# Delta-rule scan on one core: output products kept for eight chunks and summed by TensorE, rounds unrolled

## The chip, the cores and the metric

The kernel runs on one core of one Trainium2 chip. The metric is the device time of one execution in microseconds (us); lower is better. Five engines work side by side and meet only at semaphores: TensorE (PE in the profile), VectorE (DVE), ScalarE (ACT), GpSimd (POOL) and SyncE (SP, which here only issues DMAs).

## The reference

The program is a small model of several blocks: a gated-experts layer, a gated delta-rule attention, gated experts again, a prototype mixture, a helical attention and a second mixture. The change touches the recurrence of the delta-rule attention alone. For each of 2 x 16 heads it walks 2048 time steps with a 16x16 state S:

```python
def step(S, inp):
    qt, kt, vt, at, bt = inp
    v_hat = jnp.einsum('bij,bi->bj', S, kt)
    err = vt - v_hat
    S = at[:, None, None] * S + bt[:, None, None] * (kt[:, :, None] * err[:, None, :])
    o = jnp.einsum('bij,bi->bj', S, qt)
    return (S, o)
_, O = lax.scan(step, S0, (Q.swapaxes(0, 1), Kh.swapaxes(0, 1), V.swapaxes(0, 1), alpha.T, beta.T))
```

S goes from step to step, so the walk is serial; o is read out at each step and feeds nothing in the walk.

## The kernel before

Before the scan, other stages write one record of small matrices for each chunk of 8 steps (C = CHUNK = 8). With these a chunk needs only the state before it: an error vector, a triangular solve giving u, the next state, and the outputs. The scan (`delta_recurrence`) runs over 32 rounds of 64 steps (SPAN = 64), each of 8 chunks (`m` = 0 to 7), so 256 chunks. The partitions hold 2 batches x 16 heads x 4 quarters; each partition has 4 columns j of the state (JQ = 4). Records and values of a round sit in one of two buffers, `slot` 0 or 1, and a `Fori` loop on every engine runs over the 16 pairs of rounds.

**VectorE** carries the serial chain. One chunk is six links (`at` = 0 to 5), and each link is issued for two lanes of 2 columns: products `terms` from the record and the state; a reduce to `error`; products `u_terms`; a reduce to `u`; products `s_terms`; a reduce to the new `state`. The products are `tensor_tensor` with two SBUF inputs (line 1798), the reduces have one input (lines 1810, 1814, 1818). Each link counts its lane's semaphore `chain[lane]` up by one, and the next link waits for it. Between links 4 and 5 VectorE also reduces the outputs of the chunk before (`outputs`, line 1794), and those of chunk 7 after the last link of the round.

**GpSimd** forms the outputs, in four instructions a chunk, all `tensor_tensor`. The first, below called product A, is released by the state of the chunk before, the same event that releases link 0 of VectorE. The second, product B, is released by u, the same event that releases link 4:

```python
nc.gpsimd.tensor_tensor(o_terms[:, m % 2, :, :, 0:HD], state..., Q_IN part of the record, ALU.mult)   # A, line 1773
nc.gpsimd.tensor_tensor(o_terms[:, m % 2, :, :, HD:], u..., MIX part of the record, ALU.mult)        # B, line 1777
```

Each output has 16 + 8 = 24 products. Two adds fold them to 12 (`o_halves`, line 1781) and to 6 (`o_quarters`, line 1785), and VectorE reduces the 6.

**ScalarE** writes the decayed old state into `s_terms` (line 1761, once a chunk, before link 5) and copies the round's values into `terms` (line 1757). **SyncE** loads two rounds ahead: when a round's outputs are complete it issues their store (two DMAs) and then the record and values of the round that takes over the slot (four DMAs). **TensorE** has nothing in this stage. After the scan come a barrier of all engines and `delta_output`, which reads the outputs back.

## Time and profile before

| what | us |
|---|---|
| median of 3 runs | 5733.3 (5731.94 to 5738.86) |
| the profiled execution, its own time | 5734.14 |
| span of the profile | 5732.2 |
| VectorE busy over the span | 4562.1 (80%) |
| GpSimd busy over the span | 2916.3 (51%) |
| TensorE busy over the span | 3463.3 (60%) |
| ScalarE busy over the span | 2952.6 (52%) |

The shares are means over stages that have little in common. The scan is the stretch from about 918 us to 2230 us. A stretch of it is read from the timeline (each line an instruction, or several alike in a row on one engine), and the groups of instructions by line give means over all chunks.

### The profile page before, as it was taken

How to read it: one execution, taken by the hardware profiler on the slowest of the kernel's cores; microseconds unless marked ns; L12 is line 12 of the kernel's file. 1: busy time of each engine (PE TensorE's matmuls, PEld its weight loads, DVE VectorE, ACT ScalarE, POOL GpSimd, SP SyncE). 2: the span in 40 equal slices, each digit the busy share in tenths (PEclk: the TensorE clock that was granted, in tenths of full speed). 3: DMA queues.
4: the chain of work that ended last, by engine and by line, in shares of the span. 5: the costliest groups of instructions: out<-in, count | busy, mean ns of one | idle time of the engine just before them, and what ended most of it. 6: DMA issues, size and time to landing. Idle time of an engine off the chain costs nothing. (4 is left out here: it accounts for less than half of the span.)

```text
span 5732.2 us, 66648 instructions
## 1 busy us (share of the span) xinstructions
PE 3463.3 (60%) x14606; PEld 1230.7 (21%) x14606; DVE 4562.1 (80%) x8093; ACT 2952.6 (52%) x3700; POOL 2916.3 (51%) x2351
## 2 busy tenths in 40 slices
PE   7972000000000002888975899999999999999568
PEld 3330000000000001332332233333333333333123
DVE  5554776999999997553487899999999999999352
ACT  5563000101001002553445598989898988999632
POOL 1001564777777774112045366666666666666512
PEclk9996555555555556998998799999999999999889
DMA  1016324223232322000124211111111111110200
GB/s 40 11 35 119 65 25 107 64 52 66 49 66 49 66 52 76 10 14 0 58 99 166 49 35 33 32 33 33 33 32 33 32 33 34 41 37 5 80 27 30
DMA packets 143838, 275.50 MB, mean 48 GB/s; under 512 B 73808, under 2 KB 87504, under 8 KB 136336
## 3 DMA queue, kind: packets, MB, share of 16 engines
q1 hardware_dynamic: 142128, 263.57, 19.9%
q10 hardware_dynamic: 1440, 8.65, 0.4%
q8 instruction: 129, 2.11, 0.2%
q14 instruction: 141, 1.16, 0.1%
HBM read 178.65 MB, written 93.36 MB: 47 GB/s over the span
## 5 line engine op out<-in xcount | busy, mean ns | idle before, releaser
L1027 POOL TENSOR_TENSOR att_heads_rest<-att_heads_probs,att_heads_high 128x576 f16<-128x576 f32 x1024 | 1390.7, 1358 | 848.2 <-ACT att_heads_high L1114 842.1
L1144 DVE TENSOR_REDUCE att_heads_maxima<-att_heads_peek 128x1 f32<-128x512 f32 x2048 | 1311.2, 680 | 99.2 <-PE att_heads_peek L1040 72.2
L1112 ACT ACTIVATE att_heads_probs<-att_heads_scores 128x1024 f32<-128x1024 f32 x1024 | 1076.2, 1051 | 248.9 <-PE att_heads_scores L1058 240.6
L1058 PE MATMUL att_heads_scores<-att_heads_q,att_heads_k 128*128 128x512 f16 (+1 forms) x4096 | 1067.8, 382 | 34.2 <-issue 21.2
L1882 PE MATMUL delta_out_sums<-delta_out_squares,main_head_sum 128*128 128x512 f32 x32 | 16.6, 649 | 1763.4 <-ACT delta_out_squares L1911 1763.4
L1114 ACT ACTIVATE att_heads_high<-att_heads_scores 128x1024 f16<-128x1024 f32 x1024 | 1077.5, 1052 | 0.0
L1164 DVE TENSOR_TENSOR att_heads_rest<-att_heads_probs,att_heads_high 128x448 f16<-128x448 f32 x1024 | 892.0, 871 | 65.2 <-POOL att_heads_rest L1027 53.1
L1040 PE MATMUL att_heads_peek<-att_heads_k,att_heads_q 112*128 112x512 f16 x2048 | 687.9, 395 | 89.4 <-DVE att_heads_maxima L1144 47.5
L1761 ACT ACTIVATE delta_scan_s_terms<-delta_scan_state,delta_scan_record 128x64 f32<-128x64 f32 x256 | 104.7, 409 | 1160.2 <-DVE delta_scan_state L1818 1160.2
L1058 PEld LDWEIGHTS att_heads_scores<-att_heads_q,att_heads_k 128*128 128x128 f16 (+1 forms) x4096 | 395.0, 98 | 455.3 <-ACT att_heads_high L1114 38.8
L1074 PE MATMUL att_heads_out<-att_heads_high,att_heads_v_head 128*64 128x512 f16 x2048 | 418.5, 405 | 5.1 <-DVE att_heads_rest L1164 4.2
L1074 PE MATMUL att_heads_out<-att_heads_rest,att_heads_v_head 128*64 128x512 f16 x2048 | 393.9, 381 | 0.0
L1882 PEld LDWEIGHTS delta_out_sums<-delta_out_squares,main_head_sum 128*128 128x128 f32 x32 | 6.6, 211 | 1772.3 <-issue 1772.3
L1574 POOL TENSOR_TENSOR delta_chunks_terms<-delta_chunks_kq 128x256 f32<-128x256 f32 (+3 forms) x64 | 157.1, 2479 | 422.5 <-DMA delta_chunks_ab<-delta_ab 402.0
L1773 POOL TENSOR_TENSOR delta_scan_o_terms<-delta_scan_state,delta_scan_record 128x512 f32<-128x512 f32 x256 | 341.5, 1334 | 29.8 <-DMA delta_scan_vt<-delta_v 29.3
L259 PE MATMUL ffn_pre<-ffn_xn_parts,ffn_weights 128*128 128x512 f16 x1536 | 336.0, 382 | 11.5 <-POOL ffn_weights L298 11.5
L1777 POOL TENSOR_TENSOR delta_scan_o_terms<-delta_scan_u,delta_scan_record 128x256 f32<-128x256 f32 x256 | 201.4, 787 | 241.4 <-DVE delta_scan_u L1814 241.4
L1798 DVE TENSOR_TENSOR delta_scan_terms<-delta_scan_record,delta_scan_state 128x256 f32<-128x256 f32 x512 | 300.8, 626 | 18.8 <-ACT delta_scan_terms L1757 15.0
L341 DVE SCALAR_TENSOR_TENSOR main_x<-ffn_hidden,ffn_gate,main_x 128x512 f32<-128x512 f32 x256 | 194.9, 764 | 151.1 <-ACT ffn_hidden L284 151.1
L1798 DVE TENSOR_TENSOR delta_scan_s_terms<-delta_scan_record,delta_scan_u 128x256 f32<-128x256 f32 x512 | 312.9, 650 | 0.0
L1040 PEld LDWEIGHTS att_heads_peek<-att_heads_k,att_heads_q 112*128 112x128 f16 x2048 | 160.0, 96 | 647.8 <-DVE att_heads_maxima L1144 549.2
L1781 POOL TENSOR_TENSOR delta_scan_o_halves<-delta_scan_o_terms 128x384 f32<-128x384 f32 x256 | 284.3, 1110 | 20.1
(240 smaller groups left out, 5174.0 us busy)
## 6 DMA issues: line engine op xcount, KB each, us to landing
delta_scan_record<-delta_record SPq DMA_DIRECT2D x64, 1026.0 KB, 10.7
att_heads_q<-att_hel SPq DMA_DIRECT2D x192, 128.0 KB, 3.1
att_heads_k<-att_hel SPq DMA_DIRECT2D x192, 128.0 KB, 3.3
delta_record<-delta_chunks_record SPq DMA_DIRECT2D x64, 256.5 KB, 4.7
att_hel<-att_hel_high SPq DMA_DIRECT2D x32, 512.0 KB, 3.9
att_hel<-att_hel_rest SPq DMA_DIRECT2D x32, 512.0 KB, 4.5
att_o<-att_heads_out_copy SPq DMA_DIRECT2D x256, 32.0 KB
att_out_parts<-att_o ACTq DMA_DIRECT2D x8, 1024.0 KB, 14.2
```

The lines of the kernel that those rows point to most:

```text
L259: mm = nc.tensor.matmul(pre[:, k % SLOTS], weights[:, u, w_part, tile, o * P:(o + 1) * P], xn_parts[:, x_part, tile, tokens(n)], start=til ...
L1027: nc.gpsimd.tensor_tensor(rest[:, step % 4, SPLIT:], probs[:, step % 4, SPLIT:], high[:, step % 4, SPLIT:], ALU.subtract).then_inc(rest_b_ ...
L1040: nc.tensor.matmul(peek[:, m % 2], q[0:MAX_ROW, slot, 0, tile * P:(tile + 1) * P], k[0:MAX_ROW, slot, 0, tokens(blk)], start=True, stop=Tr ...
L1058: mm = nc.tensor.matmul(scores[:, step % 2, tokens(j)], k[0:rows, slot, number, tile * P:(tile + 1) * P], q[0:rows, slot, number, tokens(h ...
L1074: mm = nc.tensor.matmul(out[j * WIDE:(j + 1) * WIDE, half], v_head[:, slot, tile], part[:, step % 4, tokens(j)], start=tile == 0 and part ...
L1112: nc.scalar.activation(probs[:, step % 4], scores[:, step % 2], ACT.Exp, scale=LOGIT_SCALE).then_inc(probs_ready, 1)
L1114: nc.scalar.activation(high[:, step % 4], scores[:, step % 2], ACT.Exp, scale=LOGIT_SCALE).then_inc(high_ready, 1)
L1144: nc.vector.tensor_reduce(maxima[:, m:m + 1], peek[:, m % 2], AX.X, ALU.max).then_inc(peek_read, 1)
L1164: nc.vector.tensor_tensor(rest[:, step % 4, 0:SPLIT], probs[:, step % 4, 0:SPLIT], high[:, step % 4, 0:SPLIT], ALU.subtract).then_inc(rest ...
L1773: nc.gpsimd.tensor_tensor(o_terms[:, m % 2, :, :, 0:HD], state[:, (m - 1) % 4].unsqueeze(2).broadcast_to([P, JQ, C, HD]), table[:, Q_IN:Q_ ...
L1781: nc.gpsimd.tensor_tensor(o_halves[:, m % 2], o_terms[:, m % 2, :, :, 0:FOLD], o_terms[:, m % 2, :, :, FOLD:], ALU.add).then_inc(o_halves_ ...
L1798: return nc.vector.tensor_tensor(out, matrix.rearrange("p (r c) -> p r c", c=columns).unsqueeze(1).broadcast_to([P, JL, rows, columns]), v ...
```

## The change

GpSimd keeps only the two products. `o_terms` grows from two chunks to two rounds of eight chunks, so the 24 products of all 64 steps of a round stay in SBUF. When GpSimd has finished a round, TensorE multiplies the identity matrix with each of the 24 product slices (256 columns, 24 elements apart in SBUF, float32) and accumulates them in half a PSUM bank, `o_sum`; two banks alternate. ScalarE copies the sum to `o_out` with one instruction (`evict`), placed in its queue after the decay of chunk 4 of the next round (EVICT_AT = 4). The store of a round, and the loads that follow it in SyncE's queue, wait for that copy. The two folding adds of GpSimd and the output reduce of VectorE go. VectorE gets one wait at link 3 for GpSimd's product A of three chunks before. All `Fori` loops over pairs of rounds are written out.

```diff
--- before.py
+++ after.py
@@ -1694,14 +1694,12 @@
         u_terms = s.sb("u_terms", [P, 2, JQ, C, C])
...
         s_terms = s.sb("s_terms", [P, 2, JQ, HD, C + 1])
-        o_terms = s.sb("o_terms", [P, 2, JQ, C, HD + C])
-        FOLD = (HD + C) // 2
-        o_halves = s.sb("o_halves", [P, 2, JQ, C, FOLD])
-        o_quarters = s.sb("o_quarters", [P, 2, JQ, C, FOLD // 2])
+        o_terms = s.sb("o_terms", [P, 2, CHUNKS, JQ, C, HD + C])
+        o_sum = s.ps("o_sum", [P, 2, BLK])
         o_out = s.sb("o_out", [P, 2, JQ, SPAN])
...
         stored = [s.sem(f"stored{slot}") for slot in range(2)]
-        o_halves_ready, o_quarters_ready = s.sem("o_halves_ready"), s.sem("o_quarters_ready")
+        o_summed = s.sem("o_summed")
         chain = [s.sem(f"chain{lane}") for lane in range(LANES)]
...
         ROUNDS = T // SPAN
@@ -1709,7 +1707,7 @@
         STEP = 6
...
         C0 = BEFORE + 1
-        O_CREDIT = 2 * CHUNKS
+        EVICT_AT = 4
 
...
             for lane in range(LANES):
@@ -1729,7 +1727,7 @@
 
...
 
-                    sp.wait_ge(o_ready, (pair * 2 + slot + 1) * CHUNKS + O_CREDIT)
+                    sp.wait_ge(o_ready, pair * 2 + slot + 1)
                     for b in range(B):
...
                         sp.dma_start(dram["delta_o"][b, bass.ds(pair * 2 + slot, 1)].rearrange("r (p j) t -> (r p) (j t)", j=JQ),
@@ -1737,18 +1735,26 @@
 
...
                     load(0, slot)
-                with sp.Fori(1, ROUNDS // 2) as pair:
+                for pair in range(1, ROUNDS // 2):
                     for slot in range(2):
...
                 for slot in range(2):
-                    sp.wait_ge(stored[slot], ROUNDS // 2 * 32 + 32)
+                    sp.wait_ge(stored[slot], ROUNDS // 2 * 32)
 
...
             def _(act):
-                with act.Fori(0, ROUNDS // 2) as pair:
+                def evict(round_number):
+                    slot = round_number % 2
+                    act.wait_ge(o_summed, round_number + 1)
+                    if round_number >= 2:
+                        act.wait_ge(stored[slot], round_number // 2 * 32)
+                    nc.scalar.activation(o_out[:, slot].rearrange("p j (m t) -> p m j t", t=C),
+                                         o_sum[:, slot, 0:CHUNKS * JQ * C].rearrange("p (m j t) -> p m j t", m=CHUNKS, j=JQ), ACT.Copy).then_inc(o_ready, 1)
+
+                for pair in range(ROUNDS // 2):
                     for slot in range(2):
...
 
@@ -1760,39 +1766,43 @@
                             wait_chains(act, ((pair * 2 + slot) * CHUNKS + m) * STEP + C0)
...
                                                  scale=record[:, slot, m, DECAY:DECAY + 1]).then_inc(decayed, 1)
+                            if m == EVICT_AT and pair * 2 + slot >= 1:
+                                evict(pair * 2 + slot - 1)
+                evict(ROUNDS - 1)
+
+            @block.tensor
+            def _(pe):
+                for round_number in range(ROUNDS):
+                    slot = round_number % 2
+                    pe.wait_ge(o_terms_ready, (round_number + 1) * CHUNKS * 2)
+                    if round_number >= 2:
+                        pe.wait_ge(o_ready, round_number - 1)
+                    by_element = o_terms[:, slot].rearrange("p m j t e -> p e (m j t)")
+                    for e in range(HD + C):
+                        mm = nc.tensor.matmul(o_sum[:, slot, 0:CHUNKS * JQ * C], c["identity"][:], by_element[:, e], start=e == 0, stop=e == HD + C - 1)
+                    mm.then_inc(o_summed, 1)
 
...
             def _(pool):
-                with pool.Fori(0, ROUNDS // 2) as pair:
+                for pair in range(ROUNDS // 2):
                     for slot in range(2):
                         pool.wait_ge(loaded[slot], (pair + 1) * LOADS)
+                        if pair >= 1:
+                            pool.wait_ge(o_summed, pair * 2 + slot - 1)
                         for m in range(CHUNKS):
...
                             wait_chains(pool, number * STEP + C0)
-                            nc.gpsimd.tensor_tensor(o_terms[:, m % 2, :, :, 0:HD], state[:, (m - 1) % 4].unsqueeze(2).broadcast_to([P, JQ, C, HD]),
+                            nc.gpsimd.tensor_tensor(o_terms[:, slot, m, :, :, 0:HD], state[:, (m - 1) % 4].unsqueeze(2).broadcast_to([P, JQ, C, HD]),
                                                     table[:, Q_IN:Q_IN + C * HD].rearrange("p (t i) -> p t i", i=HD).unsqueeze(1)
...
                             wait_chains(pool, number * STEP + C0 + 4)
-                            nc.gpsimd.tensor_tensor(o_terms[:, m % 2, :, :, HD:], u[:, m % 4].unsqueeze(2).broadcast_to([P, JQ, C, C]),
+                            nc.gpsimd.tensor_tensor(o_terms[:, slot, m, :, :, HD:], u[:, m % 4].unsqueeze(2).broadcast_to([P, JQ, C, C]),
                                                     table[:, MIX:MIX + C * C].rearrange("p (t s) -> p t s", s=C).unsqueeze(1)
                                                     .broadcast_to([P, JQ, C, C]), ALU.mult).then_inc(o_terms_ready, 1)
-                            pool.wait_ge(o_terms_ready, number * 2 + 2)
-                            nc.gpsimd.tensor_tensor(o_halves[:, m % 2], o_terms[:, m % 2, :, :, 0:FOLD], o_terms[:, m % 2, :, :, FOLD:], ALU.add
-                                                    ).then_inc(o_halves_ready, 1)
-                            pool.wait_ge(o_halves_ready, number + 1)
-                            pool.wait_ge(o_ready, number + O_CREDIT - 1)
-                            nc.gpsimd.tensor_tensor(o_quarters[:, m % 2], o_halves[:, m % 2, :, :, 0:FOLD // 2], o_halves[:, m % 2, :, :, FOLD // 2:],
-                                                    ALU.add).then_inc(o_quarters_ready, 1)
 
...
             def _(dve):
-                def outputs(pair, slot, m):
-                    dve.wait_ge(o_quarters_ready, (pair * 2 + slot) * CHUNKS + m + 1)
-                    if m == 0:
-                        dve.wait_ge(stored[slot], pair * 32 + 32)
-                    nc.vector.tensor_reduce(o_out[:, slot, :, m * C:(m + 1) * C], o_quarters[:, m % 2], AX.X, ALU.add).then_inc(o_ready, 1)
-
                 def product(out, matrix, vector, rows, columns):
                     return nc.vector.tensor_tensor(out, matrix.rearrange("p (r c) -> p r c", c=columns).unsqueeze(1).broadcast_to([P, JL, rows, columns]),
@@ -1822,21 +1832,17 @@
                     dve.sem_inc(chain[lane], BEFORE)
...
                     nc.vector.memset(state[:, 3, lane * JL:(lane + 1) * JL], 0.0).then_inc(chain[lane], 1)
-                dve.sem_inc(o_ready, O_CREDIT)
-                for slot in range(2):
-                    dve.sem_inc(stored[slot], 32)
-                with dve.Fori(0, ROUNDS // 2) as pair:
+                for pair in range(ROUNDS // 2):
                     for slot in range(2):
...
                             for at in range(STEP):
+                                if at == 3 and number >= 3:
+                                    dve.wait_ge(o_terms_ready, number * 2 - 5)
                                 if at == 5:
-                                    if m >= 1:
-                                        outputs(pair, slot, m - 1)
                                     dve.wait_ge(decayed, number + 1)
                                 link(slot, m, number, at)
-                        outputs(pair, slot, CHUNKS - 1)
 
...
```

## Rows read from the trace of the kernel before

**Rows 1.** Groups by line, 930 to 2227 us: busy us, mean ns, idle before.
```profile
L1773 POOL TENSOR_TENSOR delta_scan_o_terms<-delta_scan_state,delta_scan_record 128x512 f32<-128x512 f32 x256 | 341.5, 1334 | 29.8 <-DMA delta_scan_vt<-delta_v 29.3
...
L1781 POOL TENSOR_TENSOR delta_scan_o_halves<-delta_scan_o_terms 128x384 f32<-128x384 f32 x256 | 284.3, 1110 | 20.1
...
L1777 POOL TENSOR_TENSOR delta_scan_o_terms<-delta_scan_u,delta_scan_record 128x256 f32<-128x256 f32 x256 | 201.4, 787 | 241.4 <-DVE delta_scan_u L1814 241.4
...
L1761 ACT ACTIVATE delta_scan_s_terms<-delta_scan_state,delta_scan_record 128x64 f32<-128x64 f32 x256 | 104.7, 409 | 1160.2 <-DVE delta_scan_state L1818 1160.2
```

**Rows 2.** Timeline, first chunk into the second: start, us, engine, line, idle before.
```profile
935.12 0.48 DVE L1798 TENSOR_TENSOR delta_scan_u_terms<-delta_scan_record,delta_scan_error 128x128 f32<-128x128 f32 x2
935.52 0.47 DVE L1814 TENSOR_REDUCE delta_scan_u<-delta_scan_u_terms 128x16 f32<-128x128 f32 x2
935.90 0.74 DVE L1798 TENSOR_TENSOR delta_scan_s_terms<-delta_scan_record,delta_scan_u 128x256 f32<-128x256 f32 x2
936.57 0.80 DVE L1818 TENSOR_REDUCE delta_scan_state<-delta_scan_s_terms 128x32 f32<-128x288 f32 x2
937.29 0.75 DVE L1798 TENSOR_TENSOR delta_scan_terms<-delta_scan_record,delta_scan_state 128x256 f32<-128x256 f32 x2
937.96 0.77 DVE L1810 TENSOR_REDUCE delta_scan_error<-delta_scan_terms 128x16 f32<-128x272 f32 x2
938.65 0.59 DVE L1798 TENSOR_TENSOR delta_scan_u_terms<-delta_scan_record,delta_scan_error 128x128 f32<-128x128 f32 x2
```

**Rows 3.** Timeline, chunks 6 and 7 of the first round.
```profile
964.79 0.47 DVE L1814 TENSOR_REDUCE delta_scan_u<-delta_scan_u_terms 128x16 f32<-128x128 f32 x2
965.18 1.19 DVE L1798 TENSOR_TENSOR delta_scan_s_terms<-delta_scan_record,delta_scan_u 128x256 f32<-128x256 f32 x2
965.40 0.69 POOL L1777 TENSOR_TENSOR delta_scan_o_terms<-delta_scan_u,delta_scan_record 128x256 f32<-128x256 f32 x1 [0.88 <-DVE delta_scan_u L1814]
...
967.28 1.12 DVE L1798 TENSOR_TENSOR delta_scan_terms<-delta_scan_record,delta_scan_state 128x256 f32<-128x256 f32 x2
967.38 0.73 POOL L1785 TENSOR_TENSOR delta_scan_o_quarters<-delta_scan_o_halves 128x192 f32<-128x192 f32 x1 [0.16 <-POOL delta_scan_o_halves L1781]
```

**Rows 4.** Timeline, chunk 0 of the second round and the start of chunk 1.
```profile
973.00 1.25 POOL L1773 TENSOR_TENSOR delta_scan_o_terms<-delta_scan_state,delta_scan_record 128x512 f32<-128x512 f32 x1
...
976.27 0.75 DVE L1798 TENSOR_TENSOR delta_scan_s_terms<-delta_scan_record,delta_scan_u 128x256 f32<-128x256 f32 x2
976.49 1.11 POOL L1777 TENSOR_TENSOR delta_scan_o_terms<-delta_scan_u,delta_scan_record 128x256 f32<-128x256 f32 x1 [2.24 <-DVE delta_scan_u L1814]
...
977.66 0.75 DVE L1798 TENSOR_TENSOR delta_scan_terms<-delta_scan_record,delta_scan_state 128x256 f32<-128x256 f32 x2
977.68 1.58 POOL L1781 TENSOR_TENSOR delta_scan_o_halves<-delta_scan_o_terms 128x384 f32<-128x384 f32 x1
```

**Rows 5.** Timeline, chunks 6 and 7 of the second round.
```profile
1003.63 1.27 POOL L1773 TENSOR_TENSOR delta_scan_o_terms<-delta_scan_state,delta_scan_record 128x512 f32<-128x512 f32 x1
...
1005.17 0.47 DVE L1814 TENSOR_REDUCE delta_scan_u<-delta_scan_u_terms 128x16 f32<-128x128 f32 x2
...
1010.78 0.78 POOL L1777 TENSOR_TENSOR delta_scan_o_terms<-delta_scan_u,delta_scan_record 128x256 f32<-128x256 f32 x1 [0.89 <-DVE delta_scan_u L1814]
```

**Rows 6.** Windows on float32 matmuls, L689 (256 columns): PE, PEld, clock.
```profile
2866.00:2872.00 6.00, 6.00 (x28) 4.91 (x27) 1.00 0.44 175
```

**Rows 7.** Windows on the start of the next stage's float32 matmuls, all engines.
```profile
2249.50:2253.00 3.50, 3.46 (x5) 1.56 (x6) 0.00 (x0) 0.84 (x1) 0.00 (x0) 0.53 1.13 218
```

**Rows 8.** Timeline, the last of the four load DMAs after a round.
```profile
1502.63 0.48 SPq L1728 DMA_DIRECT2D delta_scan_vt<-delta_v  x1
```

**Rows 9.** The same DMA by its tile, 1502.6 to 1503.2 us: time to landing.
```profile
DMA to landing us min/median/max: 11.0/11.0/11.0
```

**Rows 10.** Timeline, end of the scan.
```profile
2224.54 0.80 DVE L1818 TENSOR_REDUCE delta_scan_state<-delta_scan_s_terms 128x32 f32<-128x288 f32 x2
...
2225.97 0.35 DVE L1794 TENSOR_REDUCE delta_scan_o_out<-delta_scan_o_quarters 128x32 f32<-128x192 f32 x1 [0.63 <-POOL delta_scan_o_quarters L1785]
```

## The prediction

> **What bounds the kernel now.** I first read the groups by line of the scan [rows 1]. GpSimd's products A and B and the first add come 256 times at 1.33, 0.79 and 1.11 us, and the second add took 0.73 us where the timeline shows it [rows 3]: about 4 us a chunk. ScalarE's single instruction a chunk had waited 1160 us in total for VectorE's new state [rows 1]. Then the timeline: the same reduce to u of chunk 6 starts at 964.79 in one round and at 1005.17 in the next [rows 3, 5], so a round is 40.38 us and a chunk 5.05 us. All other waits being short, VectorE's chain of links sets the pace. GpSimd is no bound by its own length, but see what it does to VectorE.
>
> VectorE's chunk without disturbance can be put together from the start times of the first chunks [rows 2]: terms 937.29 to error 937.96 is 0.67, to u_terms 938.65 is 0.69, u_terms 935.12 to u 935.52 is 0.40, to s_terms 935.90 is 0.38, to state 936.57 is 0.67, to the next terms 937.29 is 0.72. That sums to 3.53 us. Against 5.05, 1.52 us a chunk is something else. The output reduce is 0.34 to 0.35 long [rows 10] and overlaps its neighbours, some 0.26. The rest, over 1.2 us, is inside VectorE's products. A pair of s_terms products takes 0.74 or 0.75 us in [rows 2, 4] but 1.19 in [rows 3], a pair of terms 0.75 against 1.12 in the same groups. The reduces don't change (0.80, 0.77, 0.47). In each long pair a GpSimd product or add started after VectorE's first of two instructions and before the second: the two engines' two-input instructions exclude each other, and the pair is longer by what is left of GpSimd's.
>
> **Who wins.** The contested moment is that in which VectorE's first instruction of a pair is done. In [rows 3] B starts 0.22 after the s_terms pair, takes its own 0.69, and the pair takes 1.19: GpSimd went between the two. Of the 256 chunks, 192 look like this, all with GpSimd idle for 0.88 us before. In [rows 4] B starts 0.22 after the pair as well, but the pair takes 0.75 and B 1.11: VectorE went through and GpSimd waited. That is so in chunk 0 of all 32 rounds, where GpSimd had been idle 2.24 us. The contest right after it also goes to VectorE: the add starts 0.02 after the terms pair, takes 1.58 and the pair 0.75 [rows 4], while the other add against a terms pair wins [rows 3].
>
> **The change, part by part.**
> 1. *Output reduce off VectorE*: 0.26 us a chunk of the chain. Its replacement is counted below.
> 2. *Both adds off GpSimd*: 1.11 and some 0.7 a chunk [rows 1, 3]. Worth nothing by themselves; but they no longer collide with the terms pair and, through the queue, no longer push A into the u_terms pair.
> 3. *A moves*. Before, it stood behind the second add. Now GpSimd waits for the state, so A is released together with the terms pair, as B is with the s_terms pair, and by the same kind of event: I put its start 0.22 after the pair, as B's. A and B both meet a pair of VectorE head on, in every chunk.
>  - Price if GpSimd wins. For B, 1.19 against 0.75 is 0.44 where B takes 0.69; where B takes 0.78 [rows 5] it is 0.09 more. The two lengths come equally often, mean 0.49. In general it is GpSimd's time less 0.25. A takes 1.25 with nothing of VectorE beside it [rows 4], and in the other chunks some 0.17 less (1.27 where it waited about 0.18 for a pair [rows 5]). With a wait of 0.05 it costs 1.05 or 0.89, mean 0.98.
>  - Price if VectorE wins. B: nothing [rows 4]. A begins its work about 0.35 later, ends 1.65 to 1.85 after the chunk's start, and the u_terms pair is due at 0.67 + 0.69 = 1.36, so it must wait. In [rows 5] A ends at 1004.90 and the reduce to u starts at 1005.17, 0.27 later; undisturbed it starts at 1.76. So 0.16 or 0.36, mean 0.27.
> 4. *TensorE*: 24 float32 matmuls of 256 columns, two passes each. A window of such matmuls has 28 passes in 6.0 us at granted clock 1.00, 0.214 each [rows 6]; 48 are 10.3 us. Each round TensorE starts after some 25 us of rest, and the next stage's first 3.5 us after a rest ran at 0.53 of the 2.4 GHz [rows 7], half clock. I take 4 us at half clock (9 passes) and 39 x 0.214 = 8.3: 12.3 us. It lies beside the next round. The copy is asked for after chunk 4's decay, some 4 chunks and 1 us on, at 19 to 21 us, so cover remains. Below, all 48 at half clock is 20.6 us. No moving operand in the trace has a stride as here (96 bytes); if it cost twice the time, 25 us.
> 5. *ScalarE's copy*: 256 elements; the decay of 64 takes 0.41 [rows 1], I estimate 0.5 us. ScalarE is idle four fifths of each chunk.
> 6. *Loads later*. Store and loads now go out after chunk 4, not at the end of the round. From the copy, six issues of about 0.5 us up to the last [rows 8], which lands 11.0 us later [rows 9]: 14 us. With 1.2 us up to the copy's end and 0.8 for the copies of values it is 16 us after chunk 4's start; four chunks are 18 us at 4.5 a chunk. Hidden; at chunks under 4.0 us it isn't.
> 7. *Waits and loops*. The new wait of VectorE at link 3 is for a product three chunks back, satisfied long before. Written-out loops remove register and branch work that the intervals of [rows 2] don't show as a bound: 0.
> 8. *Tail*. Before, the last output is done at 2225.97 + 0.35 = 2226.32, 0.98 after the last state (2224.54 + 0.80) [rows 10]. Now TensorE starts about when B ends, 1.0 before the last state, and 12.3 + 0.5 + 0.3 for handovers bring it to 12.1 after it: +11 us, once.
>
> **Sum.** The change comes down to two contests. In the new queue GpSimd is idle before B from A's end to u: if A wins, A ends 1.5 after the chunk's start and B starts 1.0 (A's delay) + 2.14 + 0.22 = 3.4 after it, 1.9 idle. That is nearer to the 2.24 of the lost contest than to the 0.88 of the won ones, so I let B lose. Then B ends late, at most 0.3 us before A's release, so A has hardly rested and wins. A chunk is 3.53 + 0.98 = 4.51, a round 36.1, against 40.4: 4.3 x 32 = 137 us less. With the tail, -126. On the profiled execution's 5734.1 that gives 5608, and 5607 on the median of 5733.3 (the two differ by 0.8). I forecast **5607 us**, chance 0.36 together with its variant: after a lost contest GpSimd loses the next as well, as in [rows 4]. Then chunks alternate between 4.51 and 3.53 + 0.27 + 0.49 = 4.29, a round is 35.2, and the time 5578.
>
> The Trainium skill (SBUF — State Buffer, "SBUF: two separate sides") says that GpSimd and two-input VectorE instructions share a port pair by an exclusive lock, which goes for the whole instruction to whoever starts first. The 192 chunks like [rows 3] agree, the 32 like [rows 4] don't: there B starts 0.11 us before VectorE's second instruction and yet waits 0.4. By that rule the change would come out as the first rival does, at 5732.
>
> **Rivals.**
> - *GpSimd wins every contest* (0.34). Each chunk is 3.53 + 0.98 + 0.49 = 5.00, a round 40.0, 0.4 x 32 = 13 us less, and the tail takes 11 back: **5732**, no change. For it: 192 contests against 32 in the very geometry. If loss belongs to chunk 0 for a reason of its own, B still loses there: 0.53 x 32 = 17 us less, **5715**. I give 0.18 to the first and 0.16 to the second.
> - *VectorE wins against A, GpSimd against B* (0.12). A's rest is 1.1 us when B wins, B's then 0.9, so if the limit of rest lies below 1.1 this is stable: 4.29 x 8 = 34.3 a round, -195 + 11: **5550**.
> - *VectorE wins both* (0.04): 3.80 a chunk, 30.4 a round, but the loads (part 6) then bind at about 31.5: -284 + 11, **5460**.
> - *TensorE late* (0.14), the one on the slow side. ScalarE's queue holds the copy ahead of the decay of chunk 5, and link 5 of VectorE waits for the decay. If the strided reads double the matmul time to 25 us, the copy waits at 21 us, the decay comes 4 us late in each round, and with contests as in the first rival that is +128: **5860**. It decides from about 21 us for the 24 matmuls. Against it: 20.6 even at half clock throughout.
>
> **How the numbers follow.** From no change I can tell about 0.2%, 11.5 us. The range from 5545 to 5740 holds the forecast and its variant, the first rival in both forms, and the second: 0.82. Its bounds also take in A's price from 0.89 to 1.05 (21 us either way over 256 chunks). The forecast's own range is 5565 to 5630. Faster by over 0.2%: 0.36 + 0.12 + 0.04 + 0.16, and a little of the 5732 case, 0.70. Same: 0.15. Slower: 0.15, the TensorE case and a little of the 5732 case.
>
> **What the profile afterwards would show.** Product A starting 0.2 after the first terms product in all chunks; the terms pair 1.6 to 1.8 us long (A won) or 0.75 (A lost, and u_terms long); the s_terms pair 0.75 with B at 1.1 (B lost) or 1.2 (B won). 24 matmuls a round over about 12 us, the copy never waiting, no DMA wait at a round's start, and about 12 us between the last state and the last copy. I am wrong if who wins is set by something other than GpSimd's rest, if A's start moves past VectorE's second instruction, if TensorE needs over 20 us a round, or if VectorE's undisturbed intervals grow.

## The result and the profile after

The changed kernel takes 5820.35 us (median of 4 runs, 5809.46 to 5822.52) where the one before took 5732.62 in the same session: a ratio of 1.0148, interval 1.0130 to 1.0166. It is 1.5% slower; forecast were 5607 us, range 5545 to 5740. The profiled execution has a span of 5820.7 us against 5732.2.

The groups by line of the scan, 930 to 2325 us, answer to [rows 1]; the columns are the same.

```profile
L1782 PE MATMUL delta_scan_o_sum<-delta_scan_o_terms,main_identity 128*128 128x256 f32 x1536 | 993.6, 838 | 843.1 <-POOL delta_scan_o_terms L1800 843.1
...
L1808 DVE TENSOR_TENSOR delta_scan_terms<-delta_scan_record,delta_scan_state 128x256 f32<-128x256 f32 x512 | 416.4, 851 | 104.5 <-ACT delta_scan_terms L1763 104.5
...
L1796 POOL TENSOR_TENSOR delta_scan_o_terms<-delta_scan_state,delta_scan_record 128x512 f32<-128x512 f32 x256 | 314.7, 1229 | 391.9 <-DVE delta_scan_state L1828 257.7 <-DMA delta_scan_vt<-delta_v 127.0 <-DVE delta_scan_terms L1808 7.2
...
L1800 POOL TENSOR_TENSOR delta_scan_o_terms<-delta_scan_u,delta_scan_record 128x256 f32<-128x256 f32 x256 | 188.2, 735 | 492.0 <-DVE delta_scan_u L1824 492.0
```

Two things stand out. TensorE is busy for 993.6 us, 31.05 a round, where I had 12.3. And VectorE, which had waited for hardly anything, now waits 104.5 us ahead of its terms. The waits over the stage say for whom (engine, line, waited for, us in total, times, longest):

```profile
ACT delta_scan_o_out L1754 <- PE delta_scan_o_sum L1782: 260.1, 32, 34.8
...
ACT delta_scan_terms L1763 <- DMA delta_scan_vt<-delta_v: 240.9, 31, 35.0
...
DVE delta_scan_terms L1808 <- ACT delta_scan_terms L1763: 104.5, 31, 14.7
...
DVE delta_scan_state L1828 <- ACT delta_scan_s_terms L1767: 5.6, 7, 1.5
```

ScalarE waits for TensorE's sum in every round (34.8 of it at the end, the other 225 us in 31 rounds), then for loads, and VectorE waits for ScalarE. The timeline of one round shows the chain, from chunk 4 into the next round:

```profile
1507.84 1.27 DVE L1808 TENSOR_TENSOR delta_scan_s_terms<-delta_scan_record,delta_scan_u 128x256 f32<-128x256 f32 x2
...
1508.06 0.77 POOL L1800 TENSOR_TENSOR delta_scan_o_terms<-delta_scan_u,delta_scan_record 128x256 f32<-128x256 f32 x1 [1.90 <-DVE delta_scan_u L1824]
...
1509.76 1.64 DVE L1808 TENSOR_TENSOR delta_scan_terms<-delta_scan_record,delta_scan_state 128x256 f32<-128x256 f32 x2
...
1509.98 1.14 POOL L1796 TENSOR_TENSOR delta_scan_o_terms<-delta_scan_state,delta_scan_record 128x512 f32<-128x512 f32 x1 [1.15 <-DVE delta_scan_state L1828]
...
1511.34 0.38 ACT L1754 ACTIVATE delta_scan_o_out<-delta_scan_o_sum 128x256 f32<-128x256 f32 x1 [6.13 <-PE delta_scan_o_sum L1782]
...
1514.80 0.60 SPq L1726 DMA_DIRECT2D delta_scan_vt<-delta_v  x1
...
1523.79 6.73 PE L1782 MATMUL delta_scan_o_sum<-delta_scan_o_terms,main_identity 128*128 128x256 f32 x10 [12.48 <-POOL delta_scan_o_terms L1800]
...
1525.56 0.75 ACT L1763 ACTIVATE delta_scan_terms<-delta_scan_vt 128x64 f32<-128x64 f32 x4 [5.47 <-DMA delta_scan_vt<-delta_v]
...
1526.34 1.15 DVE L1808 TENSOR_TENSOR delta_scan_terms<-delta_scan_record,delta_scan_state 128x256 f32<-128x256 f32 x2 [1.61 <-ACT delta_scan_terms L1763]
...
1529.11 0.78 POOL L1800 TENSOR_TENSOR delta_scan_o_terms<-delta_scan_u,delta_scan_record 128x256 f32<-128x256 f32 x1 [2.24 <-DVE delta_scan_u L1824]
```

The copy (1511.34) had waited 6.13 us for the sum. Behind it SyncE issues the store and the four loads, the last at 1514.80; ScalarE can use their values 10.8 us later, at 1525.56, and VectorE has by then waited 0.8 of its 1.61 us for the new round. From the copy's start to the values it is 14.2 us, as estimated from [rows 8, 9]; but 14.2 after a sum that takes 31 is too late. The sum of round r starts at the end of r, and the loads behind it are those of round r + 2. So two rounds take the 39.5 us of a round's chunks, less 0.95 because the sum starts before the last state is done, plus 31.05 for the sum, 14.2 from copy to values and 0.8 for ScalarE's copies of the values: 84.6, or 42.3 a round. The two rounds that end at 1526.34 took 84.7; over the stage the way from copy to the new round is 15.4 on average instead of 15.0, and a round takes 42.6.

Products: B starts 0.22 after the s_terms pair, takes 0.77, and the pair 1.27; A starts 0.22 after the terms pair, takes 1.14, and the pair 1.64. GpSimd wins both. Of the 256 s_terms pairs 254 are lengthened in their second instruction, and 218 of the terms pairs: 472 contests won. Of the other 38 terms pairs, 31 are chunk 0 of a round, where the loads release A ahead of the pair (A was 0.7 us ahead at 1526.34), and in 5 A came 0.5 us after the pair's start, too late for a contest. At 1529.11, in chunk 0, B wins after 2.24 us of rest and with A run ahead of the terms pair: the very case in which it lost in [rows 4].

The two s_terms pairs and two terms pairs that are left are contests that GpSimd lost, and all four lie in the first chunks of the first round: B in chunks 0 and 2, after 2.24 and 1.90 us of rest, and A in chunks 1 and 3, after 0.28 and 0.37. In chunks 1 to 3 of that round the winner is just the one that the prediction's variant has: a B that has rested long loses, the A behind it, which has not rested, loses as well, and then GpSimd wins twice; chunks 1 and 2 take 4.19 and 4.43 us. From B of chunk 3 on GpSimd loses no contest, whatever its rest. Here is B in chunk 2 and in chunk 4, with the same start and the same rest:

```profile
945.13 0.74 DVE L1808 TENSOR_TENSOR delta_scan_s_terms<-delta_scan_record,delta_scan_u 128x256 f32<-128x256 f32 x2
945.35 1.02 POOL L1800 TENSOR_TENSOR delta_scan_o_terms<-delta_scan_u,delta_scan_record 128x256 f32<-128x256 f32 x1 [1.90 <-DVE delta_scan_u L1824]
...
954.19 1.27 DVE L1808 TENSOR_TENSOR delta_scan_s_terms<-delta_scan_record,delta_scan_u 128x256 f32<-128x256 f32 x2
954.41 0.77 POOL L1800 TENSOR_TENSOR delta_scan_o_terms<-delta_scan_u,delta_scan_record 128x256 f32<-128x256 f32 x1 [1.91 <-DVE delta_scan_u L1824]
```

What begins in the program between the last contest that GpSimd loses (A of chunk 3) and the first that it wins against this pattern (B of chunk 4) is VectorE's new wait at link 3, which is there from chunk 3 of the first round on (`at == 3 and number >= 3`).

The windows over one sum (busy us of PE, PEld, DVE, ACT and POOL, then granted clock, DMA share, GB/s), and the end of the stage against [rows 10]:

```profile
1480.00:1511.00 31.00, 30.75 (x48) 15.46 (x48) 27.00 (x65) 2.64 (x9) 11.13 (x12) 0.50 0.08 17
```
```profile
2290.80 31.05 PE L1782 MATMUL delta_scan_o_sum<-delta_scan_o_terms,main_identity 128*128 128x256 f32 x48 [12.21 <-POOL delta_scan_o_terms L1800]
2290.95 0.80 DVE L1828 TENSOR_REDUCE delta_scan_state<-delta_scan_s_terms 128x32 f32<-128x288 f32 x2
2321.89 0.38 ACT L1754 ACTIVATE delta_scan_o_out<-delta_scan_o_sum 128x256 f32<-128x256 f32 x1 [34.78 <-PE delta_scan_o_sum L1782]
```

48 passes in 30.75 us is 0.64 each, and the granted clock stays at 0.50 of 2.4 GHz though TensorE works without a pause. The last copy ends 30.5 us after the last state, where the last output was 0.98 after it before.

The account: the last state comes at 2291.75 instead of 2225.34, 66.4 later. That is 104.5 - 15.0 us of waiting for values (15.0 is the wait at the stage's start, which both have) plus 5.6 for the decay, less about 29 by which the chunks themselves are shorter (some 20 of them in chunk 0, 4.48 us long against 5.14 in experiment 2, because A has run ahead of the pair). The tail adds 29.5: 96. The later stages took 3498 us in this profile and 3506 in the one before, which makes the 88.5 of the two spans; in the profiles of this study they lie between 3492 and 3507, and no run here explains the spread.

### The profile page after: what moved, and what is told of

It reads as the page before. It is cut to its first block and busy times, and to the rows that moved or that the text cites. A ratio compares the mean times of both kernels' runs of the same rounds, so it can differ in the third digit from the quotient of the medians.

```text
span 5820.7 us, 65636 instructions
## 1 busy us (share of the span) xinstructions
PE 4448.1 (76%) x16142; PEld 1722.4 (30%) x16142; DVE 4555.4 (78%) x7837; ACT 2958.9 (51%) x3732; POOL 2429.2 (42%) x1839
## 5 line engine op out<-in xcount | busy, mean ns | idle before, releaser
L1782 PE MATMUL delta_scan_o_sum<-delta_scan_o_terms,main_identity 128*128 128x256 f32 x1536 | 993.6, 838 | 843.1 <-POOL delta_scan_o_terms L1800 843.1
L1144 DVE TENSOR_REDUCE att_heads_maxima<-att_heads_peek 128x1 f32<-128x512 f32 x2048 | 1310.1, 679 | 92.9 <-PE att_heads_peek L1040 66.4
L1782 PEld LDWEIGHTS delta_scan_o_sum<-delta_scan_o_terms,main_identity 128*128 128x128 f32 x1536 | 494.5, 324 | 1341.9 <-POOL delta_scan_o_terms L1800 879.5
L1808 DVE TENSOR_TENSOR delta_scan_terms<-delta_scan_record,delta_scan_state 128x256 f32<-128x256 f32 x512 | 416.4, 851 | 104.5 <-ACT delta_scan_terms L1763 104.5
L1796 POOL TENSOR_TENSOR delta_scan_o_terms<-delta_scan_state,delta_scan_record 128x512 f32<-128x512 f32 x256 | 314.7, 1229 | 391.9 <-DVE delta_scan_state L1828 257.7
L1800 POOL TENSOR_TENSOR delta_scan_o_terms<-delta_scan_u,delta_scan_record 128x256 f32<-128x256 f32 x256 | 188.2, 735 | 492.0 <-DVE delta_scan_u L1824 492.0
L284 ACT ACTIVATE ffn_hidden<-ffn_pre,ffn_expert 128x512 f32<-128x512 f32 x256 | 175.5, 687 | 138.7 <-PE ffn_pre L259 136.0
## 6 DMA issues: line engine op xcount, KB each, us to landing
delta_scan_record<-delta_record SPq DMA_DIRECT2D x64, 1026.0 KB, 10.8
```

Source lines behind the costliest of these rows:

```text
L1144: nc.vector.tensor_reduce(maxima[:, m:m + 1], peek[:, m % 2], AX.X, ALU.max).then_inc(peek_read, 1)
L1782: mm = nc.tensor.matmul(o_sum[:, slot, 0:CHUNKS * JQ * C], c["identity"][:], by_element[:, e], start=e == 0, stop=e == HD + C - 1)
L1796: nc.gpsimd.tensor_tensor(o_terms[:, slot, m, :, :, 0:HD], state[:, (m - 1) % 4].unsqueeze(2).broadcast_to([P, JQ, C, HD]), table[:, Q_IN: ...
L1808: return nc.vector.tensor_tensor(out, matrix.rearrange("p (r c) -> p r c", c=columns).unsqueeze(1).broadcast_to([P, JL, rows, columns]), v ...
```

## The experiments

**1. Contiguous reads.** Only what TensorE reads is changed; the sums are of the wrong products.

```diff
-by_element = o_terms[:, slot].rearrange("p m j t e -> p e (m j t)")
+by_element = o_terms[:, slot].rearrange("p m j t e -> p (m j t e)").rearrange("p (e n) -> p e n", e=HD + C)
```

> The kernel after, with one edit: each of the 24 matmuls of a round reads 256 consecutive floats of the round's products instead of every 24th, so the sums are of the wrong products; all instructions, waits and sizes stay. Theory 1, the 96-byte stride of the moving operand makes a pass take 0.64 us: a pass falls to 0.43 us (half clock) or 0.21 (full clock), the 48 passes of a round from 30.8 us to 10 to 21, the waits of ScalarE and GpSimd for loads at the start of a round (104.5 us of VectorE's waiting) vanish, and the tail after the last state shortens by 10 to 18 us: about 5700 to 5715. Rival, a pass over 256 float32 columns with the identity costs 0.64 us whatever it reads (the clock, the weight loads): no change, 5820.

Measured: 5724.65 us, ratio 0.9993 (0.9984 to 1.0003) to the kernel before: theory 1, 10 us above its range. The windows at the start of a sum and after:

```profile
1365.00:1370.00 5.00, 4.10 (x12) 3.40 (x13) 5.00 (x13) 0.41 (x1) 2.06 (x2) 0.60 0.01 3
1370.00:1378.00 8.00, 8.00 (x38) 6.72 (x36) 8.00 (x19) 0.82 (x2) 3.59 (x4) 1.00 0.00 0
```

The clock begins at half and is full from 3.1 us on in this sum (3 to 6 us in the others); 38 passes take 8 us, 0.21 each. In the last sum the 48 passes were 12.46 us busy, the 12.3 of the prediction. VectorE waits for values at the stage's start alone (14.4 us). So the strided operand is the whole of the slowdown, and what is left of the change is worth nothing measurable.

**2. Element outermost.** A complete version of the same: the layout puts each slice of 256 together, and GpSimd writes with a long stride.

```diff
-o_terms = s.sb("o_terms", [P, 2, CHUNKS, JQ, C, HD + C])
+o_terms = s.sb("o_terms", [P, 2, HD + C, CHUNKS, JQ, C])
-nc.gpsimd.tensor_tensor(o_terms[:, slot, m, :, :, 0:HD], ...
+nc.gpsimd.tensor_tensor(o_terms[:, slot, 0:HD, m].rearrange("p e j t -> p j t e"), ...
```

> The kernel after with the products stored element by element (the 24 elements outermost, so that each slice of 256 is contiguous for TensorE and GpSimd writes with a stride of 1 KB); the result is complete. If GpSimd's time does not depend on the stride it writes with, this is as the run with contiguous reads, 5700 to 5715. Rival, GpSimd writes slower with a long stride: products A and B, 1.14 to 1.35 and 0.69 to 0.79 us now, grow, and each 0.1 us of A or B adds 26 us to the time.

Measured: 5724.88 us, 0.9995 (0.9986 to 1.0005). The means of A and B are 1.232 and 0.738 us against 1.229 and 0.735: GpSimd doesn't mind the stride it writes with. A round takes 40.07 us, the first rival's 40.0, and the time is again above the forecast range.

**3. Loads first.** TensorE stays slow; SyncE's queue is turned round.

```diff
-store(pair - 1, slot)
-load(pair, slot)
+used = (pair - 1) * 2 + slot + 1
+wait_chains(sp, used * CHUNKS * STEP + C0)
+sp.wait_ge(o_terms_ready, used * CHUNKS * 2)
+load(pair, slot)
+if used >= 2:
+    store((used - 2) // 2, (used - 2) % 2)
```

> The kernel after with SyncE's queue turned round: the loads of the round after next go out as soon as the slot's readers are done at the end of a round, and the store of the outputs follows a round later; TensorE keeps its 31 us a round. Theory 2, the slow sum costs time only because the loads are queued behind the store and so behind the sum: the 104.5 us of waiting at round starts vanish, 5716. Rival 2, the copy in ScalarE's queue ahead of the decay of chunk 5 then becomes the wait: the sum is ready 31 us into the round, link 5 of chunk 5 is due at about 29, so 2 to 3 us a round stay, 64 to 96 us: about 5790.

Measured: 5796.59 us, 1.0113 (1.0094 to 1.0131). Rival 2 is right: the waits for loads are gone, and in the waits of the stage stands instead

```profile
DVE delta_scan_state L1832 <- ACT delta_scan_s_terms L1771: 48.9, 31, 2.2
```

VectorE's link 5 of chunk 5 waits for a decay that stands behind the copy in ScalarE's queue. The slow sum has two queues behind it, the loads' and the decay's. In the kernel after, the loads come so late that each round's chunk 5 is late too, and the decay is then seldom waited for.

**4. Loads first, copy after chunk 6.** Both queues freed, `EVICT_AT = 6` on top of experiment 3.

> The kernel after (strided reads, TensorE at 31 us a round) with the loads-first queue and ScalarE's copy behind the decay of chunk 6 instead of chunk 4. If the slow sum costs time only through the two queues behind it (loads behind the store, decay behind the copy), both waits are gone now: the run with loads first alone, 5796, less its 49 us of VectorE waiting for the decay, 5748, of which about 18 are the longer tail of the strided sum. Rival, the strided reads also slow GpSimd or VectorE down by themselves: the time stays near 5796.

Measured: 5742.28 us, 1.0018 (1.0008 to 1.0028), against 5748 expected. VectorE waits for neither loads nor decays, and chunks 0 to 7 have the lengths of experiment 2. The 17 us above experiment 2 are the tail: its sum at the end is 31 instead of 12.5 us. A sum of 31 us costs nothing inside a round when nothing that VectorE needs is queued behind it. The rival, strided reads that slow GpSimd or VectorE down by themselves, is out.

**5. Strides.** 24 matmuls as before, with 256 floats 4, 8, 16 and 64 bytes apart (sums of the wrong products).

```diff
+flat = o_terms[:, slot].rearrange("p m j t e -> p (m j t e)")
+step = (1, 2, 4, 16)[round_number // 8]
-... by_element[:, e], start=...
+... flat[:, e * 64:e * 64 + (CHUNKS * JQ * C - 1) * step + 1:step], start=...
```

> The kernel after with the matmuls reading 256 floats that lie 4 bytes apart in rounds 0 to 7, 8 bytes in rounds 8 to 15, 16 bytes in rounds 16 to 23 and 64 bytes in rounds 24 to 31 (the sums are of the wrong products). Theory 1 says only that 4 bytes is fast (0.43, then 0.21 us a pass) and 96 bytes slow (0.64). If the cost comes with any stride, the last three groups all have 0.64 and a clock that stays at half; if it comes by distance, 8 bytes is still fast or in between.

Measured in one run: 5721.85 us. The windows over one sum of each group, in the order 4, 8, 16, 64 bytes:

```profile
1126.00:1140.00 14.00, 12.67 (x48) 10.44 (x48) 14.00 (x36) 1.23 (x3) 5.02 (x5) 0.85 0.00 0
```
```profile
1366.00:1380.00 14.00, 12.60 (x48) 9.99 (x48) 14.00 (x35) 1.24 (x3) 5.05 (x6) 0.88 0.01 1
```
```profile
1605.00:1628.00 23.00, 22.10 (x48) 10.71 (x48) 23.00 (x54) 2.44 (x6) 9.16 (x9) 0.93 0.00 0
```
```profile
1925.00:1947.00 22.00, 21.05 (x48) 10.76 (x48) 22.00 (x53) 2.23 (x6) 8.61 (x10) 0.91 0.00 0
```

From the starts of the passes, at granted clock 1.00, a pass takes 0.216 us at 4 bytes, 0.227 at 8, 0.453 at 16 and 0.431 at 64. So 8 bytes costs 5% and 16 or 64 bytes a factor of two. The Trainium skill (Advanced Engine Details and Errata, "SBUF Cachelines") says that reads need at least two hits in a 16-byte line to run at full speed. The four groups agree: 8 bytes apart gives two hits, 16 one.

The clock makes no difference to the two long strides. In the 16-byte group it rose to full anywhere from 3.3 to 6.1 us into the sum, and all eight sums took 22.1 us. In the stretches at granted clock 0.50 a pass takes 0.43 us at 4 and 8 bytes, and at 16 and 64 bytes just what it takes at full clock, 0.45 and 0.43. At 96 bytes, with half clock throughout, it is 0.64, one and a half times a contiguous pass at the same clock and three times one at full clock.

Inside a round the long sums cost nothing: the last state comes at 2207.23 us, against 2205.86 in experiment 1. ScalarE's copy waits in only eight rounds, 0.8 us each, and VectorE never for it. The last sum adds 8.6 us to the tail (20.5 us instead of 11.9). That the whole kernel is no slower than in experiment 1 is luck: its later stages took 3492 us, the least of all profiles.

**6. Unrolled only.** The kernel before with `range` in place of its four `Fori`.

```diff
-with dve.Fori(0, ROUNDS // 2) as pair:
+for pair in range(ROUNDS // 2):
```

> The kernel before with its four loops over pairs of rounds written out and nothing else changed. Theory 3, who wins the contest between GpSimd's product B and VectorE's s_terms pair in chunk 0 hangs on the instruction streams of the loops (register work): chunk 0 then has B at 0.78 us and the s_terms pair at 1.3 as in other chunks. Rival, it hangs on the neighbours in the queue (what GpSimd did before): B stays at 1.11 and the pair at 0.75 in chunk 0 of each round. The time moves little either way: 0.53 us x 32 = 17 us more if GpSimd wins, minus the 4 us that the loops' branches cost now; so 5745 or 5729.

Measured: 5718.69 us, 0.9977 (0.9967 to 0.9986), 12 us less than before and below both forecasts. The rival holds for the contest: the loops don't decide it. Chunk 0, timeline:

```profile
1499.19 0.74 DVE L1798 TENSOR_TENSOR delta_scan_s_terms<-delta_scan_record,delta_scan_u 128x256 f32<-128x256 f32 x2
1499.41 1.11 POOL L1777 TENSOR_TENSOR delta_scan_o_terms<-delta_scan_u,delta_scan_record 128x256 f32<-128x256 f32 x1 [2.24 <-DVE delta_scan_u L1814]
```

B still loses there. Of the 12 us, 4 are in the scan (from the first link to the last output 1288.9 us against 1292.9); the rest is outside it, within what the later stages vary by from profile to profile. Experiment 2 takes 1288.2 us for the same stretch. Against a kernel before with its loops written out, the move of the sums to TensorE is thus worth 0.7 us in these profiles, its longer tail included.

**7. B before A.** In chunks 2 and 5 of experiment 2's kernel the two products change places, so that B comes after a long rest (VectorE's wait at link 3 counts one product more to match).

```diff
+if m in (2, 5):
+    product_b(4)
+    product_a(4)
+else:
+    product_a(0)
+    product_b(4)
```

> The element-outer layout with the order of GpSimd's two products turned round in chunks 2 and 5 only, so that there B meets the s_terms pair after a rest of GpSimd of over 4 us. The contest that VectorE won in chunk 0 of the kernel before came after 2.24 us of rest; the kernel after shows GpSimd winning after 1.9. Theory 5, rest decides, with a limit between 1.9 and 2.24: B takes 1.1 and the s_terms pair 0.75 in chunks 2 and 5. Rival, not rest but what stood in the queues before: GpSimd wins as elsewhere, B 0.69 to 0.78 and the pair about 1.2.

Measured: 5680.78 us (2 runs), 0.9904 (0.9884 to 0.9924). Chunk 5, timeline:

```profile
1501.81 1.18 DVE L1818 TENSOR_TENSOR delta_scan_s_terms<-delta_scan_record,delta_scan_u 128x256 f32<-128x256 f32 x2
1502.03 0.69 POOL L1803 TENSOR_TENSOR delta_scan_o_terms<-delta_scan_u,delta_scan_record 128x256 f32<-128x256 f32 x1 [3.29 <-DVE delta_scan_u L1834]
```

After 3.29 us of rest GpSimd wins. But in chunk 2 of the first round, before VectorE's first wait at link 3, B loses after the same 3.29 us (1.03 us long, the pair 0.74). So rest decides nothing once that wait is there; before it, the outcome still goes by rest. The gain was not expected: in these two chunks A meets no pair of VectorE head on, and they take 3.98 us instead of 4.88.

**8. Both products one link later**, in the element-outer layout with loads first.

```diff
-wait_chains(pool, number * STEP + C0)
+wait_chains(pool, number * STEP + C0 + 1)
-wait_chains(pool, number * STEP + C0 + 4)
+wait_chains(pool, number * STEP + C0 + 5)
```

> The element-outer layout and the loads-first queue together, and GpSimd's two products released one link later: A when both terms products of VectorE are done (not with them), B when both s_terms products are done. Theory 4, the price of the kernel after is that each product of GpSimd meets a pair of VectorE head on and is fitted in between (about 0.93 and 0.49 us a chunk): now A begins 0.1 after the terms pair, beside the reduces to error, and only its rest (it ends near 2.0 us into the chunk, u_terms is due at 1.36) costs about 0.5; B fits beside the reduces to state and costs under 0.1. A chunk is 3.53 + 0.5 + 0.1 = 4.1 instead of 5.0, 32 x 7 = 225 us less than element_outer: about 5500. Rival, the exclusion does not explain the extra time (the reduces also suffer from GpSimd, or links wait for something else): a chunk stays near 5, 5720.

Measured: 5515.26 us, 0.9624 (0.9606 to 0.9641), 15 above the forecast of about 5500. The timeline of a chunk:

```profile
1500.31 1.28 POOL L1800 TENSOR_TENSOR delta_scan_o_terms<-delta_scan_state,delta_scan_record 128x512 f32<-128x512 f32 x1 [0.75 <-DVE delta_scan_terms L1812]
1500.78 1.16 DVE L1812 TENSOR_TENSOR delta_scan_u_terms<-delta_scan_record,delta_scan_error 128x128 f32<-128x128 f32 x2
...
1502.24 0.74 DVE L1812 TENSOR_TENSOR delta_scan_s_terms<-delta_scan_record,delta_scan_u 128x256 f32<-128x256 f32 x2
...
1503.13 0.74 POOL L1804 TENSOR_TENSOR delta_scan_o_terms<-delta_scan_u,delta_scan_record 128x256 f32<-128x256 f32 x1 [1.54 <-DVE delta_scan_s_terms L1812]
1503.64 0.85 DVE L1812 TENSOR_TENSOR delta_scan_terms<-delta_scan_record,delta_scan_state 128x256 f32<-128x256 f32 x2
```

The s_terms pair has its 0.74 back; the u_terms pair, 0.48 alone, waits for A's rest and takes 1.16; the terms pair takes 0.85 where it would take 0.75. The price of a meeting is again what is left of GpSimd's instruction, and the reduces beside the products keep their 0.77 and 0.80 us.

**9. A alone later**, first line of that edit, on experiment 2.

> The element-outer layout with product A alone released one link later; B still meets the s_terms pair. By theory 4 a chunk is 3.53 + 0.5 (A's rest against u_terms) + 0.49 (B) = 4.5, round 36.3 against 40.06, -120: about 5605. Rival as in products_late: near 5720.

Measured: 5631.03 us, 0.9811 (0.9795 to 0.9828); 26 us above the forecast. The rest of A costs the u_terms pair 0.49 or 0.68 us by chunk, 0.58 on average and not 0.5, which is 20 of the 26.

**10. A split.** As 8, with A in two instructions of one lane each:

```diff
+product_a(1, 0)
+product_a(3, 1)
+product_b(5)
```

> As products_late, with product A cut into two instructions of one lane each: the first released after the terms pair, the second after the u_terms pair. Theory 4: a half is about 0.65 us; the first fits beside the reduces to error (0.69), the second overhangs the reduces to u (0.38) by some 0.3: chunk 3.53 + 0.05 + 0.33 + 0.06 = 4.0, round 31.8, 265 us less than element_outer: about 5460. Rival: the third instruction a chunk and its start cost more than the split saves, and the time is that of products_late or more.

Measured: 5485.58 us, 0.9563 (0.9547 to 0.9579), a round of 32.5 us where 31.8 was expected, and 26 above the forecast. The second half of A reaches into the s_terms pair, which takes 1.13 us on average instead of 0.74.

**11. A split, released by lane 0 alone.**

```diff
-wait_chains(pool, number * STEP + C0 + at)
+pool.wait_ge(chain[0], number * STEP + C0 + at)   # A for lane 1 and B also wait for the lane-1 data they read
```

> The run with A split, with GpSimd's three instructions waiting for lane 0 of VectorE's pair only (each still waits for the data that it reads). GpSimd then stands ready before VectorE's second product is done and begins at the moment that product lets go, instead of some 0.25 later (the last product's end, the semaphore and the start). If exclusion is all there is and the pair's second product keeps its turn (it starts 0.33 after the first, GpSimd's instruction would start 0.5 after it), each of the three overhangs shrinks by up to 0.2 us: 0.2 to 0.4 us a chunk, 50 to 100 us: 5385 to 5435. Rival: GpSimd gets in ahead of the second product, as in the kernel after, and the pairs become 1.2 us long: 5600 or more.

Measured: **5378.62 us**, 0.9386 (0.9366 to 0.9405), 6 us below the forecast range, a round of 29.2 us:

```profile
1505.91 0.76 POOL L1804 TENSOR_TENSOR delta_scan_o_terms<-delta_scan_state,delta_scan_record 128x256 f32<-128x256 f32 x1 [0.54 <-DVE delta_scan_terms L1824]
...
1506.78 0.48 DVE L1824 TENSOR_TENSOR delta_scan_u_terms<-delta_scan_record,delta_scan_error 128x128 f32<-128x128 f32 x2
1507.13 0.64 POOL L1804 TENSOR_TENSOR delta_scan_o_terms<-delta_scan_state,delta_scan_record 128x256 f32<-128x256 f32 x1 [0.46 <-DVE delta_scan_u_terms L1824]
...
1507.57 0.81 DVE L1824 TENSOR_TENSOR delta_scan_s_terms<-delta_scan_record,delta_scan_u 128x256 f32<-128x256 f32 x2
1508.13 0.76 POOL L1812 TENSOR_TENSOR delta_scan_o_terms<-delta_scan_u,delta_scan_record 128x256 f32<-128x256 f32 x1 [0.35 <-DVE delta_scan_s_terms L1824]
```

u_terms is at its undisturbed 0.48 us of [rows 2], s_terms at 0.81 against 0.74 (0.90 in chunks 0, 3, 4 and 7). A chunk takes 3.61 or 3.70 us; 3.53 was the sum of [rows 2]. GpSimd's instructions now fill the stretches of VectorE's reduces.

## Why the prediction was wrong, step by step

- *What bounds the kernel*: right. The undisturbed chunk of 3.53 us, the exclusion of two-input instructions, and the price of a lost contest carried over: from the second round on chunks 1 and 2 of the kernel after take 4.88 us (3.53 + 0.89 + 0.44 = 4.86), experiment 11 comes within 0.1 to 0.2 of the 3.53.
- *Part 3, A moves*: A's start (0.22 after the pair) and its price were right.
- *Who wins*, the step that made 5607 out of 5732, with *part 7, waits and loops*: wrong from the fourth chunk on. I read the length of GpSimd's rest out of two cases, 0.88 and 2.24 us, and put the new wait of VectorE at link 3 at nothing, because it is satisfied long before. GpSimd won where I let it lose. In the first chunks of the kernel after, where this wait isn't yet made, the reading by rest comes true: B loses after 2.24 and 1.90 us and wins after 0.88. From the first such wait on GpSimd wins every contest, after anything from 0.88 to 2.70 us of rest. The same switch at the same chunk is in the trace of every version in which both products meet a pair of VectorE head on (experiments 1 to 5 and 7). The kernel before and experiment 6, which never make the wait, keep losing in chunk 0. So the record points to the added wait, but no run leaves it out or puts it into the kernel before, and how a wait that is already satisfied would turn the contest is open. The loops are excluded (experiment 6), rest alone is excluded (experiment 7), and so is A's running ahead of the terms pair, since it does so in chunk 0 of the kernel after, where B wins. The Trainium skill (SBUF — State Buffer, "SBUF: two separate sides") gives the ports to whichever instruction starts first. The 472 contests that GpSimd won in the kernel after agree, the four that it lost there don't. The rival that this rule went with, 5732, is what the contiguous layout comes to: 5724.88.
- *Part 4, TensorE*: the term that made it slower. 12.3 us is right for contiguous operands (12.46). I kept twice the time, 25 us, as the bound for the stride and gave it 0.14; it is 31.05. The bound doubled a time that is for the most part at full clock. The clock stayed at half, where a contiguous pass takes 0.43 us and a strided one 0.64; whether full clock would shorten the strided one no run shows.
- *Part 6, loads*: the 14 us from copy to landing were right (14.2). But the sum was computed with the copy at chunk 4's start, and the rival with a late TensorE followed only the decay in ScalarE's queue. What is queued behind the copy on SyncE was in my own part 6 and not in the rival. The decay cost 5.6 us, the loads 90 (104.5 - 15.0). Alone, the decay would have cost 49 (experiment 3). The rival's 5860 took a price of 4 us a round and nothing more at the end; measured are 2.6 more than its 40.0 a round and 18 more at the end. That the measured 5820 lies not far from 5860 is luck: the rival had the sum too short and the wrong queue.
- *Part 8, tail*: right in form. The 12.1 us forecast are 11.9 in the contiguous version (2217.78 - 2205.86) and 30.5 here.
- *Parts 1 and 2*: without TensorE's delay, taking two adds from GpSimd and a reduce from VectorE is worth nothing clear of noise (experiment 2, 0.9995). The 0.26 us of the reduce and the adds' collisions are given back by A, which now meets its pair head on. With the products put beside the reduces the same kernel is 1.9 to 6.1% faster (experiments 8 to 11). How much of that the kernel before could have had with its adds left in, no run shows.
- *Part 7, loops*: put at 0; written out they save about 4 us in the scan (experiment 6).

## What to carry to other kernels

When work is taken off an engine that shares ports with another, look at where the remaining instructions now start: released by the same event as the other engine's products, they collide in every chunk; released one link later, and in pieces that fit beside the one-input instructions, they are nearly free. When a result moves to an engine with slack, price the operand's stride first, and then follow every queue behind the consumer, the DMA queue too. Two cases that differ in several ways don't give a threshold in one of them. And look at the first few chunks by themselves: a guard such as `number >= 3` makes them an experiment that nobody had to run.

## What the runs showed of the hardware

- A float32 pass of 256 columns on TensorE takes 0.216 us at full clock with the operand's elements 4 bytes apart, 0.227 at 8, 0.453 at 16 and 0.431 at 64 bytes (experiment 5). At 16 and 64 bytes it takes the same at half clock. At 96 bytes it takes 0.64 at half clock, where 4 bytes takes 0.43. At 96 bytes the granted clock stayed at 0.50 through 31 us of unbroken work, while with 4 to 64 bytes it rose to 1.00; what 96 bytes would take at full clock no run shows.
- GpSimd's products don't depend on the stride of their output: 1.229 and 1.232 us, 0.735 and 0.738, with 4 bytes and 1 KB.
- GpSimd and VectorE excluded each other only in VectorE's two-input instructions. A GpSimd product of 1.14 us inside a pair makes the pair 1.64; beside reduces it adds nothing to them (0.77 and 0.80 throughout). So the engines of this kernel met not at semaphores alone.
- Who goes first when both stand ready is not fixed by the start times: with GpSimd's B 0.22 us after the pair and 0.11 before its second instruction, it lost in chunk 2 and won in chunk 4 of the same round, after 1.90 and 1.91 us of rest.
- GpSimd's own products come in two lengths by chunk (A 1.14 and 1.32, B 0.69 and 0.78), the longer in chunks 0, 3, 4 and 7; the cause is open.
